# Two of 25 row tiles of the relational edge stage taken by one-hot products on TensorE in place of indirect DMAs

## The chip, the cores and the metric

The kernel runs on one core of one Trainium2 chip. The metric is the device time of one execution in microseconds (us), as the median over runs. A tile here is 128 edges, one on each partition, with 64 float32 features: 128 x 64.

## The reference, cut to what matters

Four graph layers follow one another over 12,500 nodes and 400,000 edges, each with a residual and a layer norm. The change lies in the third, the relational layer. With 16 relations it computes for every edge the product of its source node's row and the 64 x 64 weight of the edge's relation, and sums these messages at the destination node:

```
h_src = feat[src]
msg = jnp.zeros((h_src.shape[0], weight.shape[2]), dtype=feat.dtype)
for r in range(num_rels):
    mask = etypes == r
    msg = msg + h_src * mask[:, None].astype(feat.dtype) @ weight[r]
out = jax.ops.segment_sum(msg, dst, num_segments=feat.shape[0])
...
x = _layernorm(x + _L2_gnn_ref(x, L2_gnn_weight, src, dst, edge_type_16), axis=-1)
```

Edges are sorted by destination, so a segment sum is a running sum along the edges that restarts where the destination changes.

## The kernel before

The stages run one after the other, each a block with its own instruction streams for TensorE (PE), VectorE (DVE), ScalarE (ACT), GpSimd (POOL) and SyncE (SP): `edges_01` and `nodes_01` (the first two layers), `edges_2` and `nodes_2` (the relational layer), `edges_3` and `nodes_3` (the last). A block ends when all its engines have.

`nodes_01` ends by writing to HBM the table `Y`: for each node and each of the 16 relations the product of the node's row and that weight, so 16 rows of 64 floats for each node. It also leaves the nodes' rows in SBUF as `k.X` (node 98 p + b at partition p, block b, 6,272 floats on a partition).

`edges_2` has 3,125 tiles: partition p holds 3,125 edges in a row, and tile t is the t-th edge of every partition. Tiles go in slots of 25 (`SL2`), slots in chunks of five (`NS2`); there are 125 slots in 25 chunks. In a slot q of a chunk c:

- ACT copies the 25 index columns and the 25 "same destination as before" flags of the slot (lines 1548 and 1549), after the slot's buffer has been read in the chunk before.
- POOL issues one indirect DMA for each tile (`gather`, line 137), which fetches row `src * 16 + relation` of `Y` for every partition into `msg[:, q, t, :]`. It waits for ACT at the slot's start and for nothing else.
- Tile 12 of slots 1 to 4 is not fetched by POOL: SP (slots 1 and 3) and ACT (slots 2 and 4) issue 128 plain row copies for it (`row_tile`, `fetch_rows`, line 159).
- DVE waits for all rows of the slot and then runs the 25 steps of the sum (line 1600): run[t] = run[t-1] * same[t] + msg[t]. Each step waits for the one before. The last slot goes in five parts of five tiles.
- SP stores the slot's 25 running sums into `R2`.

PE has nothing in this stage. The five slots of `msg`, `run` and `idx` are the buffers between POOL and DVE. After the stage `fix_rows` (from line 1152 on) repairs the seams between partitions, and `nodes_2` follows.

The names that matter: `s.link` is "signal when done and wait for that", `turns` and `Fori` are hardware loops over the chunks.

Of the kernel before, what the change touches and what calls it, by code (L numbers as in the profile page):

```python
# [12 lines left out]
P = 128  # L13
# [9 lines left out]
D = 64  # L23
# [330 lines left out]
def edges_01(nc, k, ins):  # L354


    with ExitStack() as ctx:
# [3 lines left out]
        def sem(name):  # L361
            return ctx.enter_context(nc.semaphore(name))
# [1105 lines left out]
def edges_2(nc, k, ins):  # L1468

    with ExitStack() as ctx:  # L1470
        def sb(name, shape, dt=F32):
            return ctx.enter_context(nc.sbuf_tensor(name, shape, dt))

        def sem(name):
            return ctx.enter_context(nc.semaphore(name))
# [11 lines left out]
        meta_ready, run_ready, part_ready, vsteps, zero_put = (  # L1487
            sem(s) for s in ("meta_ready2", "run_ready2", "part_ready2", "vsteps2", "zero_put2"))
        R2 = k.R2[0:E, :].rearrange("(p t) f -> p t f", p=P)
        Z = k.Z[0:E, :].rearrange("(p t) f -> p (t f)", p=P)  # L1490
        LAST = CHUNKS2 - 1
# [7 lines left out]
        def row_tile(eng, c, q):  # L1499
            eng.wait_ge(listed[q], 16)  # L1500
            eng.sem_clear(listed[q])
            fetch_rows(nc, eng, lists[:, q, :], msg[:, q, ROW_AT2, :], Yb, 4 * D, by_row[q])
            list_rows(eng, c + 1, q)

        def last_slot(c, q):
            return isinstance(c, int) and c == LAST and q == NS2 - 1
# [49 lines left out]

        @block.gpsimd
        def _(pool):
            def slot(c, q):
# [12 lines left out]
            body(LAST)  # L1572

        @block.vector
        def _(v):
            s = Steps(v, vsteps)
            s.link(v.memset(run[:, NS2 - 1, SL2 - 1, :], 0.0))

            def slot(c, q, part):
                if not is_first(c):  # L1580
                    v.wait_ge(stored[q], 16 * c)
                for t in range(SL2):
                    if t % part == 0:
                        if last_slot(c, q):
                            v.wait_ge(late[t // part], 16 * (part - (t // part == ROW_AT2 // part)))
                            if t // part == ROW_AT2 // part:
                                v.wait_ge(by_row[q], 16 * P * CHUNKS2)
                        else:
                            v.wait_ge(got[q], 16 * (SL2 - (q in BY_ROW)) * (c + 1))
# [12 lines left out]
                    if t == SL2 - 1 and part == SL2:  # L1602
                        ins_.then_inc(run_ready, 1)
                    elif t % part == part - 1:
                        ins_.then_inc(part_ready, 1)
                    else:
                        s.done(ins_)

            s.fresh()
            for q in range(NS2):  # L1610
                slot(0, q, SL2)
# [642 lines left out]
def build(nc, ins, out):  # L2254
    with ExitStack() as ctx:
# [104 lines left out]
```

## Time and profile before

| | us |
|---|---|
| median of 3 runs | 12724.05 (12720.05 to 12810.73) |
| profiled execution, its own time | 12744.54 |
| span of its trace | 12742.7 |
| POOL busy | 9537.5 (75%) |
| DVE busy | 6179.3 (48%) |
| PE busy | 2970.5 (23%) |
| mean granted TensorE clock | 0.537 of full |

The trace is one execution of the program, and the span is the time from its first to its last instruction. Busy time is the time in which an engine works on something, with issue and waits left out. POOL's indirect DMAs are counted as busy while POOL makes their descriptors; the data arrive later. The granted clock is 0.5 where TensorE runs at 1.2 GHz, and 1.0 at 2.4 GHz. A matmul in float32 appears in the trace as two instructions (a group of one matmul 128x512 is "x2").

### The profile page before, as it was taken

What the parts mean: (1) busy time and instruction counts of PE and PEld (TensorE: products, weight loads), DVE (VectorE), ACT (ScalarE), POOL (GpSimd) and SP (SyncE); (2) the same over time, 40 slices, a digit from 0 to 9 for tenths busy, and PEclk for the clock granted to TensorE, in tenths of its full rate; (3) what the DMA queues carried; (4) which work ended last, traced back from release to release, by engine and by line L of the source; (5) the groups of instructions that cost most, each with busy time, mean ns of one, the idle gap of its engine ahead of it and who ended that gap; (6) DMA issues with size and microseconds to landing.
All of it is one profiled execution on the core that took longest, in us unless ns stands there. A gap on an engine that the chain in (4) does not pass through costs nothing. (4 is left out here: it accounts for less than half of the span.)

```text
span 12742.7 us, 117881 instructions
## 1 busy us (share of the span) xinstructions
PE 2970.5 (23%) x12074; PEld 2055.6 (16%) x12074; DVE 6179.3 (48%) x21579; ACT 1252.9 (10%) x3613; POOL 9537.5 (75%) x9956
## 2 busy tenths in 40 slices
PE   2000011111100640000000000013545545545455
PEld 2000011111100320000000000012333333333334
DVE  8877477777743432222222222224555555555555
ACT  3111111111111330000000000000101001011001
POOL 7777777777777767777777777777777777777776
PEclk6555555555555775555555555555555555555556
DMA  6444444444444432222222222222222222222221
GB/s 168 120 118 116 115 127 117 118 116 118 116 119 115 127 120 74 66 66 74 66 70 66 66 66 72 68 52 55 68 67 67 67 68 67 67 67 67 67 67 49
DMA packets 766546, 1107.81 MB, mean 87 GB/s; under 512 B 277264, under 2 KB 383263, under 8 KB 765038
## 3 DMA queue, kind: packets, MB, share of 16 engines
q0 software_dynamic: 328208, 302.76, 12.8%
q1 hardware_dynamic: 257781, 569.91, 12.3%
q10 hardware_dynamic: 179944, 229.99, 6.1%
q14 instruction: 597, 4.89, 0.1%
q8 instruction: 16, 0.26, 0.0%
HBM read 548.77 MB, written 553.01 MB: 86 GB/s over the span
## 5 line engine op out<-in xcount | busy, mean ns | idle before, releaser
L137 POOL DMA_INDIRECT g<-in_edge_attr,idxs x3072 | 2955.4, 962 | 938.3 <-issue 857.1
L137 POOL DMA_INDIRECT yg<-ytab,idx x3077 | 2911.6, 946 | 949.4 <-issue 920.1
L137 POOL DMA_INDIRECT msg<-Y,idx x3025 | 2874.0, 950 | 984.8 <-issue 923.5
L1600 DVE SCALAR_TENSOR_TENSOR run<-run,same,msg 128x64 f32<-128x64 f32 x3125 | 891.0, 285 | 2910.9 <-DMA msg<-Y,idx 2803.4
L611 DVE SCALAR_TENSOR_TENSOR run<-run,sameD 128x80 f32<-128x80 f32 x3072 | 907.9, 296 | 1324.3 <-DMA g<-in_edge_attr,idxs 882.5
L2023 DVE SCALAR_TENSOR_TENSOR run<-run,same,ps 128x32 f32<-128x32 f32 x3125 | 774.7, 248 | 1584.1 <-PE ps L1917 1428.7
L1156 PE MATMUL ps<-tail,before 128*128 128x64 f32 (+2 forms) x10 | 2.8, 421 | 4456.5 <-PEq L1470 3811.3
L1901 PE MATMUL ps<-ident,zx 128*128 128x128 f32 x1564 | 524.8, 439 | 1460.6 <-DMA yg<-ytab,idx 1430.5
L2006 DVE SCALAR_TENSOR_TENSOR zx<-zx,same,zs 128x32 f32<-128x32 f32 x3124 | 793.4, 254 | 135.3 <-DVE anew L1989 28.6
L615 DVE SCALAR_TENSOR_TENSOR runS<-runS,sameS,g 128x64 f32<-128x64 f32 x3072 | 852.4, 277 | 0.1
L1000 PE MATMUL ps<-hot 128*98 128x128 bf16 x3072 | 373.1, 315 | 1816.3 <-DVE hot L718 1816.3
L2025 DVE SCALAR_TENSOR_TENSOR run<-run,anew,ps 128x32 f32<-128x32 f32 x3125 | 757.8, 242 | 0.1
L1156 PEld LDWEIGHTS ps<-tail,before 128*128 128x128 f32 x10 | 2.4, 320 | 4457.1 <-issue 4457.1
L1901 PEld LDWEIGHTS ps<-ident,zx 128*128 128x128 f32 x1564 | 416.9, 326 | 1738.6 <-DMA yg<-ytab,idx 1705.2
L1000 PEld LDWEIGHTS ps<-hot 128*98 128x98 bf16 x3072 | 332.6, 202 | 1856.9 <-DVE hot L718 1856.9
L1903 PE MATMUL ps<-ident,yg 128*128 128x128 f32 x1564 | 488.8, 416 | 0.0
L718 DVE TENSOR_TENSOR hot<-ps,digits 128x2048 bf16<-128x2048 f32 x192 | 437.4, 2278 | 0.0
L1903 PEld LDWEIGHTS ps<-ident,yg 128*128 128x128 f32 x1564 | 422.4, 329 | 0.1
L1893 PE MATMUL ps<-eaT,W1e 128*128 128x512 f32 (+1 forms) x394 | 369.4, 1036 | 141.9 <-ACT eaT L1946 130.9
L1917 PE MATMUL ps<-W3e,h 128*128 128x128 f32 x1564 | 354.7, 399 | 170.2 <-ACT h L1965 170.2
L1548 ACT COPY idx<-rel_i 128x25 int32 (+1 forms) x125 | 26.6, 213 | 3621.0 <-issue 2734.8
L1917 PEld LDWEIGHTS ps<-W3e,h 128*128 128x128 f32 x1564 | 306.4, 291 | 416.1 <-issue 412.2
(356 smaller groups left out, 5893.0 us busy)
## 6 DMA issues: line engine op xcount, KB each, us to landing
R<-run SPq DMA_DIRECT2D x390, 320.0 KB, 2.3
msg<-Y ACTq DMA_DIRECT2D x6400, 0.2 KB
msg<-Y SPq DMA_DIRECT2D x6400, 0.2 KB
R<-run SPq DMA_DIRECT2D x195, 512.0 KB, 3.0
R<-run SPq DMA_DIRECT2D x124, 800.0 KB, 5.3
v<-in_edge_attr ACTq DMA_DIRECT2D x384, 256.0 KB
yg<-ytab SPq DMA_DIRECT2D x6144, 0.1 KB
RA<-runS SPq DMA_DIRECT2D x256, 256.0 KB, 2.9
```

The costliest lines, as they stand in the source:

```text
L137: eng.indirect_dma_start(out=out, out_offset=None, in_=table, in_offset=bass.IndirectOffsetOnAxis(ap=index, axis=0)).then_inc(sem, 16)
L611: s.done(v.scalar_tensor_tensor(out=run80[:, q, t], in0=p80, scalar=sameD[:, q, t:t + 1], in1=run80[:, q, t], op0=ALU.mult, op1=ALU.add))
L615: last = v.scalar_tensor_tensor(out=runS[:, q, t], in0=pS, scalar=sameS[:, q, t:t + 1], in1=g64[:, q, t], op0=ALU.mult, op1=ALU.add)
L718: v.tensor_tensor(h[:, :, NB:], over(k.ps[:, 6, 0:P], 1, HB), over(digits[:, 1, at], 2, P), ALU.is_equal).then_inc(hot_ready, 1)
L1000: last = nc.tensor.matmul(k.ps[0:NB, which, 0:P], hot[:, i % 2, t, 0:NB], hot[:, i % 2, t, NB:], start=isinstance(c, int) and c == a and i ...
L1600: ins_ = v.scalar_tensor_tensor(out=run[:, q, t, :], in0=prev, scalar=same[:, q, t:t + 1], in1=msg[:, q, t, :], op0=ALU.mult, op1=ALU.add)
L1901: nc.tensor.matmul(ps(1, q)[0:w, g:g + P], zx[:, q, g:g + w], k.ident[:, :], start=False, stop=False)
L1903: last = nc.tensor.matmul(ps(1, q)[0:w, g:g + P], yg[:, q, g:g + w], k.ident[:, :], start=False, stop=g + P >= b)
L1917: last = nc.tensor.matmul(ps(3, q)[:, a:a + w], h2[0:w, m, a:a + P], k.W3e[0:w, 0:w], start=True, stop=True)
L2006: last = v.scalar_tensor_tensor(out=o, in0=p, scalar=same[:, q, t:t + 1], in1=zs[:, q, t * MSG:(t + 1) * MSG], op0=ALU.mult, op1=ALU.add)
L2023: s.done(v.scalar_tensor_tensor(out=run[:, q, t, 0:MSG], in0=p[:, 0:MSG], scalar=same[:, q, t:t + 1], in1=h, op0=ALU.mult, op1=ALU.add))
L2025: b = v.scalar_tensor_tensor(out=run[:, q, t, MSG:], in0=p[:, MSG:], scalar=anew[:, q, t:t + 1], in1=h, op0=ALU.add, op1=ALU.max)
```

## The change

In each slot, tiles 6 and 18 (`HOT2`) are no longer fetched from `Y`. Their messages are computed from `k.X` and the weights, both in SBUF:

1. Once, in `prepare`, `k.X` is split into three bfloat16 parts whose sum is exact; the source node of each hot edge is split into a key (node div 7) and a place within seven (node mod 7).
2. `spread_key` (PE, 2 products with the identity) puts the keys of a slot's 2 x 128 edges along the free axis; `one_hots` (DVE) compares them with the keys that each partition holds, for 14 groups of seven nodes: twice 128 x 1792 into `hot`.
3. `find` (PE): for each hot tile 14 groups x 3 parts = 42 products of a 128 x 128 one-hot and 448 columns of `k.X` (7 nodes x 64 features).
4. `pick` (DVE) multiplies the 7 found rows by a mask and reduces them to one row; `turn` (PE) transposes it, `keep_turned` (DVE) copies that.
5. `relate` (PE) multiplies it by the weights of all 16 relations, 4 products of 512 columns in float32 a slot; `pick_rel` (DVE) masks and reduces the 16 results to one and writes `msg[:, q, 6 or 18, :]`.

The buffers `hot`, `psX` (the found rows), `picked`, `rows_xT` and `psW` (the 16 results) exist once each. `HB2` is 7, `HN` is 14. DVE does `find`'s and `relate`'s followers for slots ahead of the sum: at slot n it does `pick_rel` for n, `pick` for n+1, `one_hots` for n+2 and `next_key` for n+3, then the 25 steps of the sum for n, then `keep_turned` for n+1. POOL issues 22 or 23 indirect DMAs a slot, where it issued 24 or 25.

The semaphores `got` and `added` of `edges_01` are now made in `build`; nothing else changes in that stage. The diff's core:

```diff
+HOT2 = (6, 18)
+HOTS = len(HOT2)
+HN, HB2 = 14, 7
...
@@ edges_2, pool
             def slot(c, q):
                 hold(pool, meta_ready, 2 * (NS2 * c + q + 1), k.passed)
                 for t in range(SL2):
-                    if t == ROW_AT2 and q in BY_ROW:
+                    if t in HOT2 or t == ROW_AT2 and q in BY_ROW:
                         continue
...
+        @block.tensor
+        def _(pe):
...
+            def find(c, q):
+                for u in range(HOTS):
+                    pe.wait_ge(hot_ready, HOTS * (NS2 * c + q) + u + 1)
+                    for i in range(HN):
+                        for part in parts_x:
+                            last = nc.tensor.matmul(psX[:, u, :], hot[:, u, i, :], part[:, i * HB2 * D:(i + 1) * HB2 * D],
+                                                    start=i == 0 and part is parts_x[0], stop=i == HN - 1 and part is parts_x[2])
+                last.then_inc(x_found, 1)
+
+            def turn(c, q):
+                hold(pe, x_ready, NS2 * c + q + 1, k.passed)
...
+            def relate(c, q):
+                pe.wait_ge(xT_ready, NS2 * c + q + 1)
+                for u in range(HOTS):
+                    for a in range(0, RELS * D, 512):
+                        last = nc.tensor.matmul(psW[:, u * RELS * D + a:u * RELS * D + a + 512], rows_xT[:, u * P:(u + 1) * P],
+                                                W[:, a:a + 512], start=True, stop=True)
+                last.then_inc(rels_made, 1)
+
+            def slot(c, q):
+                for work, m in ((turn, 1), (find, 2), (spread_key, 3), (relate, 1)):
+                    if within(*after(c, q, m)):
+                        work(*after(c, q, m))
...
+            def one_hots(c, q):
+                v.wait_ge(key_spread, NS2 * c + q + 1)
+                for u in range(HOTS):
+                    v.tensor_tensor(hot[:, u], over(psK[:, u * P:(u + 1) * P], 1, HN), over(place[:, :], 2, P),
+                                    ALU.is_equal).then_inc(hot_ready, 1)
+
+            def pick(c, q):
...
+                v.wait_ge(x_found, NS2 * c + q + 1)
+                s.link(v.tensor_tensor(picked[:, :, :, :], psX.rearrange("p u (b f) -> p u b f", f=D), over(mask[:, :, :], 3, D),
+                                       ALU.mult))
+                v.tensor_reduce(rows_x[:, :, :], picked[:, :, :, :].rearrange("p u b f -> p u f b"), AX.X, ALU.add)\
+                    .then_inc(x_ready, 1)
...
+            def pick_rel(c, q):
+                v.wait_ge(rels_made, NS2 * c + q + 1)
+                for u in range(HOTS):
+                    s.link(v.tensor_tensor(by_rel[:, :, :], psW[:, u * RELS * D:(u + 1) * RELS * D].rearrange("p (r f) -> p r f", f=D),
+                                           over(rmask[:, u, :], 2, D), ALU.mult))
+                    s.link(v.tensor_reduce(msg[:, q, HOT2[u], :], by_rel[:, :, :].rearrange("p r f -> p f r"), AX.X, ALU.add))
+
+            def prepare():
...
+                s.link(v.tensor_copy(parts_x[0][:, :], Xf))
+                s.link(v.tensor_tensor(rest, Xf, parts_x[0][:, :], ALU.subtract))
+                s.link(v.tensor_copy(parts_x[1][:, :], rest))
+                v.tensor_tensor(parts_x[2][:, :], rest, parts_x[1][:, :], ALU.subtract).then_inc(parts_done, 1)
+                v.wait_ge(parts_done, 1)
+                one_hots(0, 0)
+                next_key(0, 1)
+                pick(0, 0)
+                one_hots(0, 1)
+                next_key(0, 2)
+                keep_turned(0, 0)
+
+            def ahead(c, q):
+                pick_rel(c, q)
+                for work, m in ((pick, 1), (one_hots, 2), (next_key, 3)):
+                    if within(*after(c, q, m)):
+                        work(*after(c, q, m))
...
             def slot(c, q, part):
+                ahead(c, q)
+                scan(c, q, part)
+                if within(*after(c, q, 1)):
+                    keep_turned(*after(c, q, 1))
```

On PE, before, the end of `nodes_01` is followed by the repair of the seams with nothing of `edges_2` between:

```order
L1334 MATMUL ps<-w_hl,x_lh 128x512
L1202 UNCONDITIONAL_BRANCH
L1152 UNCONDITIONAL_BRANCH
L1156 MATMUL ps<-tail,before 128x64
```

Now PE has a loop over the chunks, of which one slot stands here (its rows come from line 1624, `turn`; 1614 and 1617, `find`; 1606 and 1608, `spread_key`; 1631, `relate`):

```order
L1624 MATMUL ps<-ident,rows_x 64x128 x2
L1614 ISA
L1617 MATMUL ps<-x_part,hot 128x448 x42
L1614 REGISTER_ALU
L1617 MATMUL ps<-x_part,hot 128x448 x42
L1606 REGISTER_ALU
L1608 MATMUL ps<-ident,key 128x128 x2
L1631 MATMUL ps<-W2r,rows_xT 128x512 x4
```

All 84 products of `find` for slot n+2 stand ahead of the four of `relate` for slot n+1.

On DVE, before, a slot in the loop is the sum alone:

```order
L1599 REGISTER_ALU
L1600 SCALAR_TENSOR_TENSOR run<-run,same,msg 128x64 x25
```

Now the same slot reads (1689 and 1691 are `pick_rel`, 1670 to 1679 `pick`, 1666 `one_hots`, 136 `next_key`, 1758 the sum, 1684 `keep_turned`):

```order
L1689 TENSOR_TENSOR by_rel<-ps,rmask 128x1024
L1691 TENSOR_REDUCE msg<-by_rel 128x64
L1689 TENSOR_TENSOR by_rel<-ps,rmask 128x1024
L1691 TENSOR_REDUCE msg<-by_rel 128x64
L1670 ISA
L1670 TENSOR_TENSOR mask<-seq,hot_in 128x14
L1673 REGISTER_ALU
L1673 TENSOR_TENSOR rmask<-seq,hot_rel 128x32
L1676 REGISTER_ALU
L1677 TENSOR_TENSOR picked<-ps,mask 128x896
L1679 TENSOR_REDUCE rows_x<-picked 128x128
L1664 REGISTER_ALU
L1666 TENSOR_TENSOR hot<-ps,place 128x1792 x2
...
L1758 SCALAR_TENSOR_TENSOR run<-run,same,msg 128x64 x25
L1684 COPY rows_xT<-ps 64x256
```

The sum of a slot now stands behind nine larger DVE instructions, of which the first four wait for PE's `relate`.

## Rows read from the trace of the kernel before

**Rows 1.** The page: span, 40 slices (slices 15 to 27 hold `edges_2`), costliest gather.

```profile
span 12742.7 us, 117881 instructions
...
PE   2000011111100640000000000013545545545455
...
PEclk6555555555555775555555555555555555555556
...
L137 POOL DMA_INDIRECT msg<-Y,idx x3025 | 2874.0, 950 | 984.8 <-issue 923.5
```

**Rows 2.** The stage's window: busy us (xcount) of PE, PEld, DVE, ACT, POOL; clock, DMA.

```profile
4638.50:8445.00 3806.50, 0.66 (x2) 0.50 (x2) 891.22 (x3126) 39.75 (x247) 2874.08 (x3026) 0.50 0.25 68
```

**Rows 3.** DVE's waits in the stage: us in total, times, longest.

```profile
DVE run L1600 <- DMA msg<-Y,idx: 2803.4, 128, 35.7
```

**Rows 4.** Timeline in the stage's middle: start us, us, engine, line, operation.

```profile
5599.25 0.95 POOL L137 DMA_INDIRECT msg<-Y,idx  x1 [0.30 <-issue]
...
5600.50 0.95 POOL L137 DMA_INDIRECT msg<-Y,idx  x1 [0.30 <-issue]
...
5613.17 7.99 DVE L1600 SCALAR_TENSOR_TENSOR run<-run,same,msg 128x64 f32<-128x64 f32 x25 [20.98 <-DMA msg<-Y,idx]
```

**Rows 5.** Timeline of the stage's two ends.

```profile
4638.58 0.94 POOL L137 DMA_INDIRECT msg<-Y,idx  x1 [61.29 <-ACT same L1549]
...
8437.70 1.57 DVE L1600 SCALAR_TENSOR_TENSOR run<-run,same,msg 128x64 f32<-128x64 f32 x5 [4.69 <-DMA msg<-Y,idx]
...
8444.33 0.66 PE L1156 MATMUL ps<-tail,before 128*128 128x64 f32 x2 [3811.32 <-PEq L1470]
```

**Rows 6.** PE's timeline in `nodes_01`: bfloat16 products of 512 columns, from an idle PE.

```profile
4621.30 0.61 PE L1332 MATMUL ps<-w_hh,x_hm 128*128 128x512 bf16 x1 [6.24 <-DVE x_lh L1452]
4621.70 0.63 PE L1333 MATMUL ps<-w_mm,x_hm 128*128 128x512 bf16 x1
...
4626.31 0.38 PE L1332 MATMUL ps<-w_hh,x_hm 128*128 128x512 bf16 x1
...
4626.96 0.38 PE L1332 MATMUL ps<-w_hh,x_hm 128*128 128x512 bf16 x1
```

**Rows 7.** The same products 224 us earlier, ten of them.

```profile
4397.15 0.63 PE L1332 MATMUL ps<-w_hh,x_hm 128*128 128x512 bf16 x1
...
4400.97 0.38 PE L1332 MATMUL ps<-w_hh,x_hm 128*128 128x512 bf16 x1
```

**Rows 8.** Windows around Rows 6, columns as in Rows 2; granted clock is third from last.

```profile
4616.00:4621.00 5.00, 0.00 (x0) 0.00 (x0) 3.18 (x4) 1.67 (x2) 0.00 (x0) 0.84 0.21 85
4621.30:4626.00 4.70, 4.70 (x12) 1.67 (x13) 0.00 (x0) 1.01 (x1) 0.00 (x0) 0.50 0.00 1
4627.00:4632.00 5.00, 5.00 (x25) 2.02 (x24) 0.00 (x0) 3.81 (x5) 0.00 (x0) 1.00 0.78 310
```

**Rows 9.** Weight loads of two float32 instructions in a row at 2.4 GHz.

```profile
4409.42 0.19 PEld L1312 LDWEIGHTS ps<-catT,W1a 128*128 128x128 f32 x1 [0.24 <-ACT catT L1366]
...
4409.85 0.19 PEld L1312 LDWEIGHTS ps<-catT,W1a 128*128 128x128 f32 x1 [0.24 <-issue]
```

**Rows 10.** Groups of DVE instructions, by size: xcount | busy us, mean ns.

```profile
L1431 DVE TENSOR_TENSOR y<-ps,cat 128x448 f32<-128x448 f32 x26 | 16.2, 623 | 54.6 <-PE ps L1317 54.6
L1189 DVE TENSOR_REDUCE st<-sq 128x7 f32<-128x448 f32 x26 | 16.1, 620 | 0.9
...
L1449 DVE TENSOR_TENSOR rest<-x2T,x_hm 128x896 f32<-128x896 f32 x13 | 14.2, 1093 | 43.2 <-ACT x_lh L1399 43.2
...
L1450 DVE CAST x_hm<-rest 64x896 bf16<-64x896 f32 x13 | 8.1, 624 | 0.4
...
L1190 DVE TENSOR_SCALAR std_in<-st 128x7 f32<-128x7 f32 x26 | 4.4, 170 | 0.9
...
L718 DVE TENSOR_TENSOR hot<-ps,digits 128x2048 bf16<-128x2048 f32 x192 | 437.4, 2278 | 0.0
```

**Rows 11.** One register instruction on DVE's sequencer: ns min/median/max.

```profile
L718 DVEq FUSED_REGOPS  x184: 57/57/64, 1649.6 to 3532.6; - x184
```

More of the change, by code:

```diff
@@ L1503, in row_tile, with after, within @@
             list_rows(eng, c + 1, q)
+        def after(c, q, m):
+            return c + (q + m) // NS2, (q + m) % NS2
+        def within(c, q):
+            return not (isinstance(c, int) and c >= CHUNKS2)
         def last_slot(c, q):
@@ L1572, in _, with spread_key @@
             body(LAST)
+        @block.tensor
+        def _(pe):
+            W = k.W2r[0:D, :, :].rearrange("i r o -> i (r o)")
+            def spread_key(c, q):
+                pe.wait_ge(keyed, NS2 * c + q + 1)
+                for u in range(HOTS):
+                    last = nc.tensor.matmul(psK[:, u * P:(u + 1) * P], key[:, u:u + 1].to_broadcast([P, P]), k.ident[:, :],
+                                            start=True, stop=True)
+                last.then_inc(key_spread, 1)
+            def find(c, q):
[9 more added lines that the diff above has]
+                for u in range(HOTS):
+                    last = nc.tensor.transpose(psT[:, u * P:(u + 1) * P], rows_x[:, u, :], k.ident[:, :])
+                last.then_inc(x_turned, 1)
+            def relate(c, q):
[9 more added lines that the diff above has]
+                        work(*after(c, q, m))
+            spread_key(0, 0)
+            pe.wait_ge(parts_done, 1)
+            find(0, 0)
+            spread_key(0, 1)
+            turn(0, 0)
+            find(0, 1)
+            spread_key(0, 2)
+            relate(0, 0)
+            for q in range(NS2):
+                slot(0, q)
+            with pe.Fori(1, LAST) as c:
+                for q in range(NS2):
+                    slot(c, q)
+            for q in range(NS2):
+                slot(LAST, q)
@@ new lines, in keep_turned @@
+            def keep_turned(c, q):
+                v.wait_ge(x_turned, NS2 * c + q + 1)
+                v.tensor_copy(rows_xT[:, :], psT).then_inc(xT_ready, 1)
+            def pick_rel(c, q):
+                v.wait_ge(rels_made, NS2 * c + q + 1)
+                for u in range(HOTS):
+                    s.link(v.tensor_tensor(by_rel[:, :, :], psW[:, u * RELS * D:(u + 1) * RELS * D].rearrange("p (r f) -> p r f", f=D),
+                                           over(rmask[:, u, :], 2, D), ALU.mult))
+                    s.link(v.tensor_reduce(msg[:, q, HOT2[u], :], by_rel[:, :, :].rearrange("p r f -> p f r"), AX.X, ALU.add))
@@ new lines, in prepare @@
+            def prepare():
+                Xf = k.X[:, :, :].rearrange("p b f -> p (b f)")
+                rest = run[:, :, :, :].rearrange("p q t f -> p (q t f)")[:, 0:NB * D]
+                rel = hot_rel[:, :, :]
+                at = (slice(None), slice(None), slice(HOT2[0], HOT2[1] + 1, HOT2[1] - HOT2[0]))
+                s.done(v.tensor_copy(hot_src[:, :, :], k.src_i[:, 0:T].rearrange("p (n t) -> p n t", t=SL2)[at]))
+                s.done(v.tensor_copy(rel, k.rel_i[:, :].rearrange("p (n t) -> p n t", t=SL2)[at]))
+                v.wait_ge(seqs_made, 2)
+                s.done(v.tensor_copy(seq[:, :], seq_i[:, :]))
+                s.done(v.tensor_copy(place[:, :], place_i[:, :]))
+                s.wait(s.n)
+                s.link(v.tensor_scalar(hot_key[:, :, :], hot_src[:, :, :], 1.0 / HB2, -3.0 / HB2, ALU.mult, ALU.add))
+                s.link(v.tensor_scalar(hot_key[:, :, :], hot_key[:, :, :], 1.5 * 2.0 ** 23, None, ALU.add))
+                s.link(v.tensor_scalar(hot_key[:, :, :], hot_key[:, :, :], -1.5 * 2.0 ** 23, None, ALU.add))
+                next_key(0, 0)
+                s.done(v.scalar_tensor_tensor(out=hot_in[:, :, :], in0=hot_key[:, :, :], scalar=-1.0 * HB2, in1=hot_src[:, :, :],
+                                              op0=ALU.mult, op1=ALU.add))
+                s.done(v.scalar_tensor_tensor(out=rel, in0=hot_src[:, :, :], scalar=-1.0 * RELS, in1=rel, op0=ALU.mult, op1=ALU.add))
+                s.link(v.tensor_copy(parts_x[0][:, :], Xf))
[9 more added lines that the diff above has]
+                keep_turned(0, 0)
@@ L1584, in slot @@
                         if last_slot(c, q):
-                            v.wait_ge(late[t // part], 16 * (part - (t // part == ROW_AT2 // part)))
+                            fetched = [i for i in range(t, t + part) if i not in HOT2 and i != ROW_AT2]
+                            v.wait_ge(late[t // part], 16 * len(fetched))
                             if t // part == ROW_AT2 // part:
@@ L1607, in slot @@
                         s.done(ins_)
+            prepare()
+            s.link(v.memset(run[:, NS2 - 1, SL2 - 1, :], 0.0))
             s.fresh()
@@ L2330, in build @@
         k.row_got = [ctx.enter_context(nc.semaphore(f"row_got{r}")) for r in range(RING)]
+        k.left_got = [ctx.enter_context(nc.semaphore(f"got{q}")) for q in range(NQ)]
+        k.added = [ctx.enter_context(nc.semaphore(f"added{q}")) for q in range(NTAB)]
         edges_01(nc, k, ins)
```

35 lines of the change are left out of this document (30 added, 5 removed).

## The prediction, as it was made before the change ran

> **What bounds the kernel now.** I read the page first: PE is idle at 1.2 GHz through the middle of the run, and the gathers of `msg` are POOL's work there, 3,025 of them at 950 ns each [rows 1]. The stage's own window then tells what limits it: of 3806.5 us POOL is busy in 2874, DVE in 891, PE in practically nothing [rows 2]. POOL's idle time is nearly all issue, 923.5 us over 3,024 gaps [rows 1], so POOL waits for nobody after the start: gathers begin 1.25 us apart, 0.95 busy and 0.30 issue [rows 4]. DVE waits 2803 us for gathered rows [rows 3], and its 25 steps take 8.0 us a slot [rows 4]. Thus a slot costs 24.2 gathers x 1.252 = 30.3 us (3,025 gathers over 125 slots), and the stage is POOL's list from 4638.6 on, up to the last step of the sum at 8439.3 and the next PE instruction at 8444.3: 3805.7 us [rows 5].
>
> **What is removed.** 250 gathers, 22.2 left a slot: POOL's pace becomes 22.2 x 1.252 = 27.8 us. Were POOL still the bound, that would be worth 250 x 1.252 = 313 us. ACT's, SP's and the row copies' work is the same, and lies beside this.
>
> **What is added: a second loop, through PE and DVE.** In the new order `one_hots` for slot n+3 stands behind `pick` of n+2 and `pick_rel` of n+1; `pick_rel` of n+1 waits for `relate` of n+1, which stands behind the 84 products of `find` for n+2; and those waited for `one_hots` of n+2. With one buffer each, no step overlaps the next: from one `find` to the next lie find, spread_key, relate, pick_rel, pick, and half of one_hots. Its length, in us:
>
> - *find at 2.4 GHz.* Back to back, 512 bfloat16 columns start 0.217 apart (three from 4626.31 to 4626.96) [rows 6], at a granted clock of 1.00 [rows 8], weight load hidden. For 448 columns 0.217 x 448/512 = 0.19; 84 of them 15.9.
> - *find's cold start.* PE will have been idle for 8 us and more of DVE work. In the rows an idle PE had lost the 2.4 GHz clock before 6.2 us were over: the window of the gap averages 0.84, the next 0.50 [rows 6, 8]. The burst then ran at half pace for 5.0 us (4621.3 to 4626.3) once, 3.8 us another time [rows 6, 7]. Half of that is lost: 1.9 to 2.5; I take 2.2.
> - *spread_key and relate.* A float32 instruction of 512 columns takes 0.43 at 2.4 GHz [rows 9], and a float32 matmul is two. Relate: 8 x 0.43 = 3.4. Spread_key: 4 instructions of 128 columns, 4 x 0.11 = 0.4. The last product's results come 0.2 later (0.38 long against 0.217 apart) [rows 6]; the two hand-overs I take at 0.1 together.
> - *pick_rel.* DVE takes 0.62 for 448 elements, 1.09 for 896 and 2.28 for 2048, from PSUM or SBUF, product or reduction alike [rows 10]. On that line 1024 elements are 1.22. Four instructions, each 0.04 behind the last: 5.0. All reductions here read with a stride that no row shows; bounds below.
> - *pick.* Two small masks (0.17 for a small one [rows 10]; 0.45 for both with gaps), product and reduction of 896 at 1.09 + 0.04 each: 2.7.
> - *one_hots, first half.* 1792 elements from PSUM into bfloat16, just as the row of 2048: 2.0 + 0.05. The second half, the sum and `keep_turned` lie beside `find`: 2.1 + 8.0 + 0.4 is less than 18. If `find` took under 10.5, the sum would be late next.
> - *Register instructions* between waits on DVE, 57 ns each [rows 11], four or so: 0.2 (between 0 and 0.5).
>
> Sum: 15.9 + 2.2 + 3.4 + 0.4 + 0.2 + 0.1 + 5.0 + 2.7 + 2.1 + 0.2 = **32.2 to 32.3**, taken as 32.3. That is longer than POOL's 27.8 and than the 30.3 of now: POOL's saving of 313 us is all hidden, as it will run five slots ahead and then wait.
>
> **A rule against the first term.** The rows have 512 columns every 0.217 us at 2.4 GHz with a new weight load each. The Trainium skill (TensorE: Matmul & The Clock Gate, "Back-to-back issue gap") says that in a real stream of weight loads and matmuls the spacing at N = 512 is about 131 ns, and that 216 is the isolated gap. By it, `find` would take 84 x 0.131 = 11.0 and the loop 27.4. This case's trace has 0.217 in exactly such a stream; the measurement decides, and the term stands.
>
> **Start and end.** `prepare`: some 12 small instructions, 3.5; two casts of 6,272 elements at the half price of the row of casts (0.62 for 896), 3.4 each, and two differences at 6.6 [rows 10]: 20.0. Then, in line, half of one_hots 2.0, find 18.3, product and reduction 2.3, half of one_hots 2.1, find 18.3, spread and relate 4.1. Slot 0's `pick_rel` begins after 71 us. From there 123 slots x 32.3 = 3973. Slot 123: pick_rel 5.0, pick 2.7, sum and copy 8.3, relate at 1.2 GHz 7.0: 23. Slot 124: pick_rel 5.0, sum 8.0, and 5.0 to the next stage as before: 18. Stage: 71 + 3973 + 23 + 18 = 4085 against 3806: **+279 us**. No other stage changes. On the profiled execution's 12744.5 that gives 13,024; the median of the runs is 20.5 lower, so **13,003 us**.
>
> **Rivals.**
> 1. *The clock stays at 2.4 GHz over the gap*, helped by the two transposes of `turn` in it. Each loop is 2.2 shorter, 30.1, and relate at the end 3.4 cheaper: 279 - 2.2 x 125 - 3.4, or nothing, 12,725. Against it: the clock had gone in a gap of 6.2 us [rows 6, 8], and this one is 10. For it: one such gap shows little of all. Chance 0.12.
> 2. *POOL stays the bound: faster.* It decides once the PE and DVE loop is under POOL's 27.8, that is 4.5 shorter than I make it. A product of 448 columns every 0.135 us or less would do it. Then 12,724 - 313 = 12,411. The Trainium skill's 131 ns (the page and section above) would just give this. Rows 6 speak against it. DVE cannot give 4.5 by itself unless its products ran at the pace of casts, which the rows of the same kind do not. Chance 0.05.
> 3. *PE never leaves 1.2 GHz*, as in most of the last stage's slices with PE half busy [rows 1]. Find, spread and relate double, and the slow start is in that: 15.9 + 3.8 - 2.2 = 17.5 more, 49.8 a slot. 123 x 17.5 = 2,150 more than the forecast: 15,150. Against it: dense bursts of 10 us and more did rise after 4 or 5 [rows 6 to 8]. Chance 0.03.
> That the change doesn't do what it says is excluded by the order of instructions.
>
> **The numbers.** Forecast 13,003 with chance 0.80. Its own bounds, a slot: cold start 1.7 to 2.8 for 2.2; registers and hand-overs -0.2 to +0.5; DVE's seven large steps on the path, three of them strided reductions and all of sizes that no row has, -0.4 to +0.6; together about -1.2 to +1.3 of 32.3, times 123: 12,855 to 13,163. That holds most of 0.80; the rest is widened by little on the low side, toward rival 1: **12,850 to 13,165**. About 1% (127 us) is what a measurement of this kernel tells from no change. Faster by more: 0.05 (rival 2). Within: rival 1 and the forecast's lowest edge, 0.15. Slower: 0.80.
>
> **What would show it.** In the stage's window PE should be busy some 22 of 32 us, POOL about 0.65 of the window, and POOL should now wait, at slot starts, for ACT's `same`, and ACT for DVE's sum. DVE's longest waits should be those of `pick_rel` for PE's `relate`, and none for gathered rows. In each slot the first ten or so products of `find` should stand 0.37 apart, the rest 0.19. The loop is right if the sum's first steps lie 32.3 apart. I am wrong by a term if the products' spacing, the 1.22 of `pick_rel`, or the length of the slow start differs; wrong in kind if DVE waits for `msg` by DMA, or if `find` starts fast.

## The result, and the profile after

The changed kernel takes 13,234.52 us (median of 4 runs, 13,230.64 to 13,238.34); the kernel before, beside it, 12,722.05. The ratio is 1.0385 with a 95% interval of 1.034 to 1.043. It is slower, as forecast, but by 512 us and not by 279, and outside the range of 12,850 to 13,165. The profiled execution of after has a span of 13,232.1 us, 489 us more than that of before.

The page of after, the same rows as [rows 1] and the changed groups (line numbers have moved: 1617 is `find`, 1631 `relate`, 1689 and 1691 `pick_rel`, 1677 and 1679 `pick`, 1666 `one_hots`, 140 the gathers):

```profile
PE   2000011111101866666666666663555455444555
...
POOL 7777777777777676666666666647777777777776
PEclk6555555555555977877877887875555655555556
...
L140 POOL DMA_INDIRECT msg<-Y,idx x2775 | 2650.4, 955 | 1547.1 <-issue 828.4
...
L1617 PE MATMUL ps<-x_part,hot 128*128 128x448 bf16 x10500 | 2309.1, 388 | 176.0 <-DVE hot L1666 176.0
...
L1689 DVE TENSOR_TENSOR by_rel<-ps,rmask 128x1024 f32<-128x1024 f32 x250 | 306.2, 1225 | 1558.6 <-PE ps L1631 1554.3
...
L1691 DVE TENSOR_REDUCE msg<-by_rel 128x64 f32<-128x1024 f32 x250 | 467.9, 1872 | 8.6
```

PE is now busy for 0.6 of each of the stage's slices, and the clock swings between its levels (slices at 0.7 to 0.9 are a mean of the two). POOL's idle time before gathers has risen from 984.8 [rows 1] to 1547.1 us while the gathers became fewer: it waits. What it waits for is told by the waits in the stage's middle, from 4800 to 8800 us (us in total, times, longest):

```profile
DVE by_rel L1689 <- PE ps L1631: 1464.3, 118, 12.6
...
PE ps L1624 <- DVE rows_x L1679: 1140.8, 117, 9.9
...
POOL msg L140 <- ACT same L1573: 717.6, 59, 18.1
```

DVE waits for PE's `relate` once a slot, PE for DVE's `pick` once a slot, each for 10 to 13 us, and DVE no longer waits for gathered rows at all, where it was 2803 us before [rows 3]. POOL waits at slot starts for ACT, and ACT for DVE's sum. That is the predicted loop. One turn of it, in the timeline (DVE first, then PE; start us, us):

```profile
5998.30 1.87 DVE L1691 TENSOR_REDUCE msg<-by_rel 128x64 f32<-128x1024 f32 x1
6000.20 1.22 DVE L1689 TENSOR_TENSOR by_rel<-ps,rmask 128x1024 f32<-128x1024 f32 x1
6001.46 1.87 DVE L1691 TENSOR_REDUCE msg<-by_rel 128x64 f32<-128x1024 f32 x1
6003.45 0.17 DVE L1670 TENSOR_TENSOR mask<-seq,hot_in 128x14 f32<-128x14 f32 x1
...
6003.80 1.09 DVE L1677 TENSOR_TENSOR picked<-ps,mask 128x896 f32<-128x896 f32 x1
6004.92 1.66 DVE L1679 TENSOR_REDUCE rows_x<-picked 128x128 f32<-128x896 f32 x1
6006.49 3.94 DVE L1666 TENSOR_TENSOR hot<-ps,place 128x1792 bf16<-128x1792 f32 x2
...
6031.16 1.23 DVE L1689 TENSOR_TENSOR by_rel<-ps,rmask 128x1024 f32<-128x1024 f32 x1 [12.43 <-PE ps L1631]
```

```profile
6006.72 0.61 PE L1624 MATMUL ps<-ident,rows_x 128*64 128x128 f32 x2 [9.72 <-DVE rows_x L1679]
6008.57 18.48 PE L1617 MATMUL ps<-x_part,hot 128*128 128x448 bf16 x84 [1.24 <-DVE hot L1666]
6026.89 0.61 PE L1608 MATMUL ps<-ident,key 128*128 128x128 f32 x4
6027.42 3.70 PE L1631 MATMUL ps<-W2r,rows_xT 64*128 64x512 f32 x8
```

The four steps of `pick_rel` begin 1.26 us before the first row, at 5997.04, so the turn is 6031.16 - 5997.04 = 34.1 us: pick_rel 6.4, pick 3.1, half of one_hots 2.0, find 18.3, spread_key and relate 4.3. Between the first product of `pick_rel` and the next slot's, over the stage's middle, the mean is 34.13 us, the shortest 34.11 and the longest 34.25. The products are as the rows of before price them (1.22 and 1.09 us). The reductions are not: 1.87 and 1.66 us, where [rows 10] gave 1.22 and 1.09.

### The profile page after: what moved, and what is told of

Read it like the earlier page. It is cut to its first block and busy times, and to the rows that moved or that the text cites. A ratio compares the mean times of both kernels' runs of the same rounds, so it can differ in the third digit from the quotient of the medians.

```text
span 13232.1 us, 144783 instructions
## 1 busy us (share of the span) xinstructions
PE 5873.5 (44%) x24297; PEld 3440.4 (26%) x24324; DVE 7878.6 (60%) x23092; ACT 1253.4 (9%) x3613; POOL 9302.1 (70%) x9708
## 5 line engine op out<-in xcount | busy, mean ns | idle before, releaser
L140 POOL DMA_INDIRECT msg<-Y,idx x2775 | 2650.4, 955 | 1547.1 <-issue 828.4
L1617 PE MATMUL ps<-x_part,hot 128*128 128x448 bf16 x10500 | 2309.1, 388 | 176.0 <-DVE hot L1666 176.0
L1617 PEld LDWEIGHTS ps<-x_part,hot 128*128 128x128 bf16 x10500 | 1103.8, 106 | 1382.6 <-issue 385.3
L1689 DVE TENSOR_TENSOR by_rel<-ps,rmask 128x1024 f32<-128x1024 f32 x250 | 306.2, 1225 | 1558.6 <-PE ps L1631 1554.3
L2166 DVE SCALAR_TENSOR_TENSOR zx<-zx,same,zs 128x32 f32<-128x32 f32 x3124 | 792.2, 254 | 135.1 <-DVE anew L2149 27.8
L1624 PE MATMUL ps<-ident,rows_x 128*64 128x128 f32 x250 | 75.8, 407 | 1210.0 <-DVE rows_x L1679 1210.0
L1666 DVE TENSOR_TENSOR hot<-ps,place 128x1792 bf16<-128x1792 f32 x250 | 493.0, 2014 | 0.0
L1691 DVE TENSOR_REDUCE msg<-by_rel 128x64 f32<-128x1024 f32 x250 | 467.9, 1872 | 8.6
L1631 PE MATMUL ps<-W2r,rows_xT 64*128 64x512 f32 x1000 | 465.7, 606 | 7.6 <-DVE rows_xT L1684 7.6
L341 PE MATMUL ps<-ident,X 128*128 128x128 f32 x224 | 50.2, 417 | 905.7 <-DVE X L326 899.2
```

The source lines that it names most:

```text
L140: eng.indirect_dma_start(out=out, out_offset=None, in_=table, in_offset=bass.IndirectOffsetOnAxis(ap=index, axis=0)).then_inc(sem, 16)
L1617: last = nc.tensor.matmul(psX[:, u, :], hot[:, u, i, :], part[:, i * HB2 * D:(i + 1) * HB2 * D], start=i == 0 and part is parts_x[0], stop ...
L1666: v.tensor_tensor(hot[:, u], over(psK[:, u * P:(u + 1) * P], 1, HN), over(place[:, :], 2, P), ALU.is_equal).then_inc(hot_ready, 1)
L2166: last = v.scalar_tensor_tensor(out=o, in0=p, scalar=same[:, q, t:t + 1], in1=zs[:, q, t * MSG:(t + 1) * MSG], op0=ALU.mult, op1=ALU.add)
```

## The experiments

Experiments 1 and 2, and a first run each of the kernels of experiments 4 and 8, ran on another chip of the same kind than all the rest; there the kernel before takes 18,436 us. In the traces taken there single instructions wait where nothing in the profile holds them, as in these rows of PE in experiment 2 (2.27 us between two of the 84 products of one `find`; elsewhere such products start 0.37 or 0.19 apart). SP and ACT issue most of their row copies 0.32 us apart there as elsewhere, but 9 to 15 in a hundred follow 2.4 to 3.0 us behind the one before, where it is 2 in a hundred in the traces of before and after:

```profile
9001.01 0.53 PE L1617 MATMUL ps<-x_part,hot 128*128 128x448 bf16 x1 [2.27 <-issue]
9003.81 0.53 PE L1617 MATMUL ps<-x_part,hot 128*128 128x448 bf16 x1 [2.27 <-issue]
```

Its times are not compared with the others. The durations of single DVE instructions are the same there (in the kernel of experiment 4 the products and reductions of `pick` and `pick_rel` agree within 0.01 us), and only these are used. On the chips of the other experiments the kernel before took 12,723 and 12,731 us, so differences between kernels of different experiments are good to some 10 us.

**1. What the reductions cost.** The kernel before, with eleven DVE instructions four times each while DVE waits for the first rows (`src`, `dst` and `out` in SBUF, `pp` in PSUM; three of the eleven stand here, cut at the dots):

```diff
+  s.link(v.tensor_reduce(out[:, 0:64], src[:, :].rearrange("p (f r) -> p f r", r=16), AX.X, ALU.add))
+  s.link(v.tensor_reduce(out[:, 0:64], src[:, :].rearrange("p (r f) -> p f r", r=16), AX.X, ALU.add))
+  ...
+  s.link(v.tensor_tensor(dst[:, :].rearrange("p (f r) -> p r f", r=16), pp.rearrange("p (r f) -> p r f", r=16), ...
```

Expected:

> The kernel before, with eleven DVE instructions of 1024 elements run four times each in the time in which DVE waits for the first rows of the stage: reductions of contiguous runs (64 sums of 16, 128 of 8), of strides of 64, 128, 16 and 2 elements, from SBUF and one from PSUM, and products with a contiguous and a strided write or read. PE is idle there. Theory A: contiguous ones 1.22 us, the one with stride 64 1.87. Rival B: contiguous 64 sums of 16 already 1.87. Rival D (PE or POOL at work beside it slows the reduction in the changed kernel): stride 64 takes 1.22 here, as PE is idle. The time of the kernel stays at 12,722 plus at most 20 us, as the instructions fill about 60 us of which 35 are waiting time and POOL is five slots ahead.

Measured: 18,535 us in one run, which says nothing beside the 18,297 to 18,577 us of the kernel before there. Its rows (ns min/median/max) do. In order: reduction of contiguous runs of 16; of a stride of 64 elements; of contiguous runs of 8; of strides of 128 and 16; of stride 2; product from PSUM, all contiguous; the same with a strided write to SBUF; with a strided read of PSUM; with a strided read of SBUF; reduction from PSUM with stride 64:

```profile
L1582 DVE TENSOR_REDUCE m_out<-m_src x4: 1220/1220/1220, 5775.0 to 5826.2; 128x64 f32<-128x1024 f32 x4
L1583 DVE TENSOR_REDUCE m_out<-m_src x4: 1865/1866/1866, 5776.3 to 5827.5; 128x64 f32<-128x1024 f32 x4
L1584 DVE TENSOR_REDUCE m_out<-m_src x4: 1220/1220/1221, 5778.2 to 5829.4; 128x128 f32<-128x1024 f32 x4
L1585 DVE TENSOR_REDUCE m_out<-m_src x4: 1870/1870/1872, 5779.4 to 5830.7; 128x128 f32<-128x1024 f32 x4
L1586 DVE TENSOR_REDUCE m_out<-m_src x4: 1857/1858/1860, 5781.3 to 5832.6; 128x16 f32<-128x1024 f32 x4
L1587 DVE TENSOR_REDUCE m_out<-m_src x4: 1220/1220/1220, 5783.2 to 5834.4; 128x64 f32<-128x1024 f32 x4
L1588 DVE TENSOR_TENSOR m_dst<-ps,m_src x4: 1224/1224/1225, 5784.5 to 5835.7; 128x1024 f32<-128x1024 f32 x4
L1589 DVE TENSOR_TENSOR m_dst<-ps,m_src x4: 1869/1873/1873, 5785.7 to 5837.0; 128x1024 f32<-128x1024 f32 x4
L1590 DVE TENSOR_TENSOR m_dst<-ps,m_src x4: 1225/1225/1225, 5787.6 to 5838.9; 128x1024 f32<-128x1024 f32 x4
L1591 DVE TENSOR_TENSOR m_dst<-m_src x4: 1898/1899/1899, 5788.9 to 5840.1; 128x1024 f32<-128x1024 f32 x4
L1592 DVE TENSOR_REDUCE m_out<-ps x4: 1224/1224/1225, 5790.8 to 5842.1; 128x64 f32<-128x1024 f32 x4
```

For 1024 elements the price goes by the stride in SBUF: 1.22 us for neighbours and for every second element, 1.86 to 1.90 us when a reduction reads every 16th, 64th or 128th, or a product reads every 64th or writes every 16th. Reading PSUM with a stride of 64 costs nothing. The number of sums doesn't matter (B falls). PE is idle here, and POOL makes descriptors beside the contiguous and the strided ones alike, so neither makes the difference (D falls as the cause); with PE at work beside it, in the kernels of experiment 4, the strided reduction took 1.91 us, some 0.05 more.

The same trace shows what the product of two SBUF operands (line 1591) does to POOL. A gather beside it took 2.58 us, and 1.80, 1.79 and 1.80 in the other three rounds, where beside the other ten instructions it took 0.94 to 0.96:

```profile
5787.73 0.95 POOL L137 DMA_INDIRECT msg<-Y,idx  x1 [0.30 <-issue]
5788.90 1.90 DVE L1591 TENSOR_TENSOR m_dst<-m_src 128x1024 f32<-128x1024 f32 x1
5788.99 2.58 POOL L137 DMA_INDIRECT msg<-Y,idx  x1 [0.30 <-issue]
```

**2. The stride moved from the reductions to the products.**

```diff
-  s.link(v.tensor_tensor(by_rel[:, :, :], psW ... "p (r f) -> p r f" ...
-  s.link(v.tensor_reduce(msg[:, q, HOT2[u], :], by_rel[:, :, :].rearrange("p r f -> p f r"), AX.X, ALU.add))
+  s.link(v.tensor_tensor(by_rel[:, :, :].rearrange("p f r -> p r f"), psW ... "p (r f) -> p r f" ...
+  s.link(v.tensor_reduce(msg[:, q, HOT2[u], :], by_rel[:, :, :], AX.X, ALU.add))
```

Expected:

> The changed kernel with by_rel and picked laid out so that the three reductions of a slot read neighbouring elements; the products before them write with a stride instead. Theory A (the reductions are dear because they read with a stride of 64 elements): the two of 1024 fall from 1.87 to about 1.22 us, the one of 896 from 1.66 to 1.09, the slot from 34.1 to about 32.3 us, and the time by 125 x 1.87 = 234 us to about 13,000. Rival B (a reduction costs this with so many short sums, 64 of 16 or 128 of 7, whatever the stride): no reduction changes, 13,234. Rival C (a stride costs as much in writing as in reading): the reductions fall and the products rise by as much, 13,234.

Measured on the slower chip: 19,331 us, 1.048 (1.040 to 1.056) of before there. Its DVE rows, from 7000 to 13,000 us, decide it, and they say C:

```profile
L1689 DVE TENSOR_TENSOR by_rel<-ps,rmask 128x1024 f32<-128x1024 f32 x210 | 391.8, 1866 | 3533.8 <-PE ps L1631 2887.2 <-remote 643.0
L1691 DVE TENSOR_REDUCE msg<-by_rel 128x64 f32<-128x1024 f32 x210 | 256.2, 1220 | 7.1
```

The 0.65 us has gone from the reduction into the product. The product of 896 in `pick`, which now writes with a stride of 7 elements, takes 1.75 us for 1.09 before.

**3. The stride moved into PSUM.** The products read PSUM with the stride and write SBUF contiguously; `by_rel` and `picked` are laid out for it (cut at the dots):

```diff
-  v.tensor_tensor(by_rel[:, :, :], psW ... "p (r f) -> p r f" ..., over(rmask[:, u, :], 2, D), ALU.mult)
+  v.tensor_tensor(by_rel[:, :, :], psW ... "p (r f) -> p f r" ..., over(rmask[:, u, :], 1, D), ALU.mult)
+  for u in range(HOTS):
+      ins_ = v.tensor_tensor(picked[:, u], psX[:, u].rearrange("p (b f) -> p f b", f=D), over(mask[:, u], 1, D), ALU.mult)
```

Expected:

> The changed kernel with the two products of 1024 and the product of 896 (now two of 448) reading PSUM with the stride and writing SBUF contiguously, so that the reductions read contiguously too. The eleven prices say: strided SBUF access 1.87, strided PSUM read 1.22. Theory A (the stride in SBUF is what the prediction missed): pick_rel is 4 x 1.22 in place of 2 x (1.22 + 1.87), pick gives back 0.57 less 0.2 for the split; the slot is 34.1 - 1.65 = 32.5 us, the time 13,234 - 206 = 13,030. Part of it may be given back if find starts earlier but the clock rises no earlier: half of 1.65 at most, 13,130. Rival: the loop is set by something else, 13,234.

Measured: 12,973.96 us, 1.0185 (1.0145 to 1.0226) of before (12,722.98 beside it): 260 us less than the changed kernel. All four steps of `pick_rel` now take the 1.22 us that the prediction read off [rows 10]; two of them:

```profile
6045.46 1.22 DVE L1690 TENSOR_TENSOR by_rel<-ps,rmask 128x1024 f32<-128x1024 f32 x1 [11.90 <-PE ps L1631]
6046.72 1.22 DVE L1692 TENSOR_REDUCE msg<-by_rel 128x64 f32<-128x1024 f32 x1
```

The slots' mean is 32.1 us (118 slots), 2.1 less. DVE's steps give 1.8 of it, where 1.65 was expected; `find` gives the rest, 18.2 us in the mean for 18.5 (from 17.4 to 19.0). With reductions at 1.22 and 1.09 us the forecast was 13,003 and a slot 32.3 us: that is this kernel, within 30 us. **This shows the strided reductions to be the term that was mis-sized.**

**4. The clock held up in the gap.** 80 products of 256 columns after each `relate`:

```diff
+  for _ in range(FILL):      # 80
+      nc.tensor.matmul(k.ps[:, 3, 2 * P:4 * P], parts_x[0][:, 0:P], parts_x[1][:, 0:2 * P], start=True, stop=True)
```

Expected:

> The changed kernel with 80 products of 256 columns after each relate, in the time in which PE waits for DVE, into columns that nobody reads. Theory: the clock stays at 2.4 GHz, find takes 15.9 to 16.1 us in place of 18.5, the slot 31.6, the time 12,925. Rival: find stays at 18.5, 13,234. Rival: the filler overruns the gap, above 13,234.

Measured: 13,084.07 us, 1.0272 (1.0231 to 1.0313), so 150 us less than the changed kernel and not 310. `find` took 16.1 us in 45 slots and 17.8 in nearly all others, 17.2 in the mean; between the filler and `find` PE was still idle for 2.5 us, in two pieces around `turn`. The same kernel had run on the slower chip as well, 19,271 us, 1.046 (1.039 to 1.054) of before there, which says nothing on the clock. For that run was expected:

> The changed kernel with 80 products of 256 columns (bfloat16, into unused columns of a PSUM bank that nobody reads then; their results are used by nobody) after each relate, so that PE works through the 9.7 us in which it waited for DVE. Theory: the clock stays at 2.4 GHz, find takes 15.9 to 16.1 us in place of 18.5, the slot 34.1 - 2.5 = 31.6, and the time 125 x 2.5 = 310 us less, 12,925. Rival: the clock is not lost in the gap or the slow start has another cause, find stays at 18.5 and the time at 13,234. Rival: the filler runs over the gap and delays turn and find, slower than 13,234.

Then that hole was filled too, with 90 products after `relate` and 6 after `turn`.

Expected:

> As the kernel with 80 filler products, but with 90 of them after each relate and 6 of 448 columns after each turn, so that the hole of 2 us before find is filled as well. With 80, find took 16.1 us in some slots and 17.8 in others. Theory (the clock is lost in the wait for DVE, and that is the whole of find's slow start): find is 16.1 in every slot, the slot 34.1 - 2.4 = 31.8 us, the time 13,234 - 295 = 12,940. Rival (something else slows find's start): still 17.8 in many slots, 13,084.

Measured: 13,001.88 us, 1.0212 (1.0197 to 1.0226), 233 us less than the changed kernel. In its middle 3,000 us (PE, PEld, DVE, ACT, POOL busy, granted clock, DMA) and in one `find`:

```profile
5000.00:8000.00 3000.00, 2940.95 (x18133) 1834.13 (x18131) 1933.57 (x3451) 30.69 (x188) 1971.82 (x2082) 1.00 0.21 63
```

```profile
6038.84 16.06 PE L1618 MATMUL ps<-x_part,hot 128*128 128x448 bf16 x84 [0.33 <-DVE hot L1672]
```

The clock is 1.00 in this window, `find` 16.1 us in 120 of 125 slots, for 18.5: the slow start costs 2.4 us a slot, where the prediction had 2.2. The slots' mean is 32.13 us, not 31.8. One slot in nearly every chunk of five took 33.4 us in the mean (22 of 118): there PE stood still for 1.7 us before `turn`, with its filler done and its rows ready, and nothing in the profile holds it. Why stays open.

```profile
5042.24 0.38 PE L1625 MATMUL ps<-ident,rows_x 128*64 128x128 f32 x2 [1.73 <-issue]
```

**5. The gathers kept.** POOL fetches all rows again and the sum uses them; PE and DVE do all the new work for a tile that nobody reads:

```diff
-  if t in HOT2 or t == ROW_AT2 and q in BY_ROW:
+  if t == ROW_AT2 and q in BY_ROW:
-  s.link(v.tensor_reduce(msg[:, q, HOT2[u], :], by_rel ...
+  s.link(v.tensor_reduce(spare[:, :], by_rel ...
```

Expected:

> The changed kernel with the 250 gathers kept, so that the sum uses the gathered rows, and all the new work on PE and DVE kept too, its result written to a tile that nobody reads. POOL's pace is 24.2 x 1.252 = 30.3 us a slot again. Theory (POOL runs under the loop of 34.1): the time is the changed kernel's, 13,234, within 20 us. Rival (the saved gathers still give part of their 313 us): up to 13,547.

Measured: 13,253.75 us, 1.0422 (1.0371 to 1.0473), and slots of 34.13 us, the same as the changed kernel's. POOL still waits for ACT, 319 us in 3,000:

```profile
POOL msg L140 <- ACT same L1574: 319.0, 33, 11.1
```

The 250 gathers that the change saves are worth nothing under this loop, within the 20 us between the two medians.

**6. The gathers left out, nothing in their place.** The kernel before, with the messages of tiles 6 and 18 counted as zero, so its sums are not the layer's:

```diff
-  if t == ROW_AT2 and q in BY_ROW:
+  if t in (6, 18) or t == ROW_AT2 and q in BY_ROW:
```

Expected:

> The kernel before without the 250 gathers and with nothing in their place (the messages of tiles 6 and 18 are left out and count as zero). It prices the saving alone: 250 x 1.252 = 313 us, 12,409. Rival (POOL's list is not what sets the stage, or its pace rises): less than 313.

Measured: 12,420.60 us beside 12,730.93, 0.9756 (0.9742 to 0.977): 310 us, for 313 expected. So much the saving is worth where POOL is the bound.

**7. A shorter `find`, and one hot tile.** Two ways to bring the loop under POOL's pace:

```diff
-  for part in parts_x:
+  for part in parts_x[:1]:
```

Expected:

> The changed kernel with only the first of the three bfloat16 parts in find, 28 products in place of 84 (this leaves out the two smaller parts of each row found). The loop is 34.1 - 56 x 0.19 = 23.5 us, under POOL's 27.8. Theory (the longer of the two loops sets the slot): POOL waits for nobody, slots are 27.8 us, the time is 12,722 - 313 = 12,409, plus some 20 for the last slots. Rival (each us taken off PE comes back as a us): 13,234 - 125 x 10.6 = 11,900.

```diff
-HOT2 = (6, 18)
+HOT2 = (6,)
```

Expected:

> The changed kernel with one hot tile a slot (6) and tile 18 gathered again. The loop: find 42 x 0.19 + 2.5 = 10.5, spread and relate 2.1, pick_rel 3.1, pick 1.8, one_hots 2.0, hand-overs 0.4: 20. POOL: 23.2 x 1.252 = 29.0 us a slot. Theory: POOL is the bound, the saving is that of 125 gathers, 156 us: 12,566. If I have the loop wrong by over 9 us: above 12,722.

Measured: 12,459.64 us with one part, 0.9787 (0.9774 to 0.9801), and 12,592.23 us with one hot tile, 0.989 (0.9876 to 0.9904), both beside 12,730.93. Slots are 28.0 and 29.05 us (expected 27.8 and 29.0), POOL's own pace. With one hot tile the saving is 139 us of 156, with one part 271 of 313. Of what is missing, some 18 us in each is at the stage's start, and shows in the changed kernel as well: while DVE casts and subtracts `k.X` in `prepare`, three gathers take 21 us in place of 3.

```profile
4631.11 3.83 POOL L140 DMA_INDIRECT msg<-Y,idx  x1 [0.30 <-issue]
4631.41 3.42 DVE L1711 CAST x_part<-X 128x6272 bf16<-128x6272 f32 x1
4634.86 6.69 DVE L1712 TENSOR_TENSOR run<-X,x_part 128x6272 f32<-128x6272 f32 x1
4635.25 9.88 POOL L140 DMA_INDIRECT msg<-Y,idx  x1 [0.30 <-issue]
4641.59 3.43 DVE L1713 CAST x_part<-run 128x6272 bf16<-128x6272 f32 x1
4645.05 6.69 DVE L1714 TENSOR_TENSOR x_part<-run,x_part 128x6272 bf16<-128x6272 f32 x1
4645.44 7.12 POOL L140 DMA_INDIRECT msg<-Y,idx  x1 [0.30 <-issue]
```

The first of the three lies beside a cast alone and ends 0.1 us behind it; the third lies beside a subtraction alone and ends 0.8 us behind it. With one part 24 us more are missing at the end, where POOL waits 34 us for the stage's last slots in place of the 10 of experiments 6 and 8.

**8. The loop opened.** Nothing is left out and no buffer added; only the order changes. Each half of `hot` is released as soon as `find` is done with it, DVE makes the next one-hots first, and `spread_key` stands ahead of `find`:

```diff
-  for work, m in ((turn, 1), (find, 2), (spread_key, 3), (relate, 1)):
+  for work, m in ((turn, 1), (spread_key, 3), (find, 2), (relate, 1)):
...
-  pick_rel(c, q)
-  for work, m in ((pick, 1), (one_hots, 2), (next_key, 3)):
+  for work, m in ((one_hots, 2), (next_key, 3), (pick, 1)):
...
+  pick_rel(c, q)
...
+  if q or not is_first(c):
+      v.wait_ge(x_found, HOTS * (NS2 * c + q - 1) + u + 1)
   v.tensor_tensor(hot[:, u], over(psK ...
```

Expected:

> The changed kernel with the serial loop opened: each half of hot is overwritten as soon as find for the slot before is done with it, DVE does one_hots, pick, pick_rel in this order, spread_key stands ahead of find. Theory: the loop is 25 us, below POOL's 27.8; POOL waits for nobody and the time is 12,722 - 313 = 12,409, perhaps 20 more for the start. Rival (PE's and DVE's work costs the time in whatever order): above 12,722.

Measured: 12,430.38 us, 0.9779 (0.9726 to 0.9832), beside 12,722.98: 293 us faster than before, 804 faster than the change. Slots are 27.7 us in the mean. DVE waits for gathered rows again, and POOL for almost nobody, some 2 us in the stage:

```profile
POOL msg L140 <- issue: 845.4, 2770, 0.3
...
POOL msg L140 <- ACT same L1573: 1.5, 2, 1.2
```

```profile
DVE run L1760 <- DMA msg<-Y,idx: 704.6, 117, 9.2
```

The difference to 313 is, within 2 us, the 18 us of `prepare`. On the slower chip the same kernel was 0.981 (0.975 to 0.987) of before, for which was expected:

> The changed kernel with the serial loop opened: one_hots for slot n+2 overwrites each half of hot as soon as find for n+1 is done with that half, DVE does one_hots, pick, pick_rel in this order, and spread_key stands ahead of find on PE. No buffer is added. Between two finds then lie one half of one_hots 2.0, pick 3.2, turn and spread_key 1.3, while relate runs beside: 18.5 + 6.5 = 25 us, below POOL's 27.8. Theory (the loss comes from the loop through PE and DVE being longer than POOL's pace): POOL is the bound again, slots are 27.8 us, POOL waits for nobody, and the time is 12,722 - 313 = 12,409, perhaps 20 more for the start. Rival (PE's and DVE's work takes the time however it is ordered, or DVE is full): the time stays above 12,722.

The reordered kernel beats both others, and its gain is 18 us short of that of the kernel that does nothing for the two tiles (6).

## Why the prediction was wrong

**What bounds the kernel now: right.** POOL's list, at 1.252 us a gather, is the stage; leaving 250 out is worth 310 us (experiment 6), forecast 313.

**The second loop: right in kind.** The order of steps, one buffer each, and the release order gave a loop through PE and DVE longer than POOL's pace. POOL waits for ACT, ACT for the sum, DVE no longer for rows; kept gathers cost nothing (5), and with the loop opened or shortened the saving appears (7, 8).

**The terms of the loop**, forecast against after: `find` with its slow start 18.1 against 18.3; `spread_key`, `relate`, the last product's results and the hand-overs 4.1 against 4.3; half of `one_hots` 2.1 against 2.0; `pick` with its masks 2.7 against 3.1; `pick_rel` 5.0 against 6.4, and 0.2 for register instructions that did not show as a term of their own. **The step that failed is the price of DVE's reductions**: "product or reduction alike", 1.22 us for 1024 elements, with "All reductions here read with a stride that no row shows". They took 1.87, 1.87 and 1.66 us: 2 x 0.65 + 0.57 = 1.87 us a slot, or 230 us over 123 slots. The prediction saw that none of its rows had the stride and bounded it by +0.6; the bound was a third of what came. The other differences lie between -0.2 and +0.2 us a slot and cancel, which is luck.

The bounds were also added up wrong. As listed, -0.5, -0.2 and -0.4 make -1.1 and +0.6, +0.5 and +0.6 make +1.7, where the prediction has -1.2 and +1.3. With +1.7 the upper edge would be 13,212, still under the 13,234.5 measured. A doubling of the three instructions (3.5 us) as the bound would have held the result.

The groups of [rows 10] read neighbouring elements, but strided ones could be had: the sort at the start of the program has them in the trace of before. Lines 222 and 224 take two operands of 256 elements in SBUF: 0.42 us where they lie in runs of two or more neighbours, and 0.60 to 0.67 us in the two steps that read and write every fourth element. Line 210 takes 512 elements, 0.69 us for neighbours and for every second element alike:

```profile
61.31 0.42 DVE L222 SCALAR_TENSOR_TENSOR X<-X 128x256 f32<-128x256 f32 x1
...
103.05 0.61 DVE L222 SCALAR_TENSOR_TENSOR X<-X 128x256 f32<-128x256 f32 x1
...
118.81 0.69 DVE L210 TENSOR_TENSOR X<-X 128x512 f32<-128x512 f32 x1
```

The rows are, in order, neighbours, every fourth and every second element. The Trainium skill (SBUF — State Buffer, "Door 1: The DMA port swizzle") says that an access which crosses to a new line of 16 bytes pays a penalty, so that float32 may stride by up to four elements for free. The runs agree that there is such an edge, with stride 2 free and strides of 7, 16 and more at 1.5 to 1.6 times the contiguous price; the trace of before has stride 4 on the dear side, 0.61 us for 0.42, and the measurement decides. The Trainium skill gives no figure for the penalty there.

**The sum of the stage.** Start 71 us forecast, 70.0 in the trace (first gather at 4629.8, first `pick_rel` at 4699.8); 123 slots 3,973 against 4,198; the last two 41 against 42. All of the miss is in the slots. The stage grew by 504 us and the span by 489, as this execution began the stage 9 us earlier and took 6 us less behind it; no run here shows a cause for these.

**The rivals.** That the clock stays up over the gap did not happen: in after, the first 13 products of `find` stand 0.37 us apart. Its price was nearly right, 2.4 us a slot for 2.2 when it is made to happen (4). That POOL stays the bound did not happen; experiments 7 and 8 show that it does once the loop is shorter than POOL's pace, and experiments 3 to 5 that it does not with loops of 32 to 34 us. No kernel here has a loop just above 27.8. The spacing of 131 ns for 512 columns, which the prediction took from the Trainium skill (TensorE: Matmul & The Clock Gate, "Back-to-back issue gap"), is not seen: 84 products of 448 columns took 16.06 us at 2.4 GHz, 0.19 each, as the trace of before had it. That PE never leaves 1.2 GHz did not happen: the granted clock averages 0.80 in the stage.

## What to carry to other kernels

Before work is moved to idle engines, write the loop through its buffers: with one buffer each, as here, the steps of two engines add up, and their sum has to be under the pace of the engine that is relieved; opening the loop by order alone turned 512 us lost into 293 gained. Price a DVE instruction by size and by stride, look through the whole trace for a row with the stride, and put a needed transposition on the PSUM side of a product, where it cost nothing.

## What the runs showed of the hardware

- DVE, 1024 float32 elements: 1.22 us contiguous or with stride 2; with strides in SBUF 1.86 to 1.87 us for a reduction (16, 64 and 128 elements), 1.87 for a product that writes with 16 and 1.90 for one that reads with 64; 1.22 us when PSUM is read with a stride of 64 (experiment 1). With smaller strides: 896 elements written with stride 7 took 1.75 us for 1.09 (experiment 2), and 256 elements with stride 4 took 0.61 us for 0.42 (trace of before).
- POOL's indirect DMAs take 3.8 to 9.9 us each in place of 0.95 while DVE casts or subtracts 6,272 elements in SBUF (experiment 7), each kind by itself too: 3.83 us beside a cast, 7.12 beside a subtraction. Beside a product of two SBUF operands they took 1.8 to 2.6 us, and beside a product with one operand in PSUM 0.95 (experiment 1). The Trainium skill (SBUF — State Buffer, "Who interferes with whom") says that casts can take the ports that DVE shares with GpSimd, and that a tensor_tensor with both inputs in SBUF takes only their read side, from which it infers that such an instruction leaves the making of descriptors alone. The traces agree on casts and not on the second: POOL was held up beside both.
- TensorE's clock fell in a wait of 10 us for DVE and rose again some 5 us into `find` (13 products of 84 at half pace); filler in the wait kept the granted clock at 1.00. Idle pieces of 2.5 us in all after 9 us of filler still cost it in 77 of 122 slots (experiment 4).
- One chip ran the three kernels that also ran elsewhere 1.45 to 1.47 times as long (before, and those of experiments 4 with 80 products and 8), with waits of 2.3 us between instructions that nothing in the profile holds. What slows it there stays open.
